# One turn number for every piece of work in place of one lag for each kind: 16 sequences through two transformer-like layers

## The chip, the cores and the metric

One core of a Trainium2 chip runs the whole program. The metric is device time in microseconds from launch to the last store. Three runs of the kernel before gave 691.0, 694.92 and 696.01 us, median 694.92.

## The reference, cut to what matters

Sixteen sequences of 128 tokens and 256 channels pass one after another, independent of each other, through two layers, all in f32.

```
# layer 0: self attention, cross attention over the encoder states, MLP
x = x + attention(qkv(ln1(x)), mask_self) @ w_ao + b_ao          # 16 heads of 16
x = x + attention(q(ln2(x)), kv(enc), mask_cross) @ w_co + b_co
x = x + gelu(ln3(x) @ w1 + b1) @ w2 + b2                          # 256 -> 1024 -> 256
# layer 1: a recurrent layer with 32 heads of 8 channels and an 8 x 8 state for each head
xn = ln(x); sx = token_shift(xn)
w, k, v, r, g = five mixtures of xn and sx, each through its own product
for each token t:                                                  # 128 steps
    a = k[t] (outer) v[t]
    out[t] = r[t] . (u * a + s);  s = a + exp(-exp(w[t])) * s
x = x + (group_norm(out) * gn_w + gn_b) * silu(g) @ Wo.T
x = x + sigmoid(xr @ Wr.T) * (square(relu(xk @ Wk.T)) @ Wv.T)     # xk, xr: mixtures of ln(x) and its shift
```

## The kernel before

All weights and all sixteen sequences lie in SBUF. The work of one sequence is cut into 223 pieces, functions that each issue a few instructions of one engine with the semaphore waits that they need: `a_...` pieces are the two attentions (arg 0 is self, 1 is cross), `b_...` pieces are the MLP and the products of the recurrent layer up to its inputs, `d_...` pieces are the recurrence, its norm, and the last gated MLP. Names carry an argument, as `a_maxima (1, 2)`: cross attention, head group 2.

Each of the engines (SP is the DMA queue, then PE, DVE, ACT, POOL) works through a static list. Its order is software pipelined over sequences: `SP_ORDER` (L87), `PE_ORDER` (L89), `DVE_ORDER` (L100), `ACT_ORDER` (L119), `POOL_ORDER` (L133) each hold (piece, argument, lag), and in round i of `for i in range(B + LAG)` every entry issues its piece for sequence i - lag, if there is such a sequence. So one order holds for all rounds; the first and last rounds are the same list with entries left out. Six or so sequences are in flight at once. An engine executes in its list's order, so a piece that waits holds up all that stand behind it.

A few pieces differ at the ends. Values are spread over the 8 state rows through DRAM for sequences 0 to 13 (`LAST = 2`), and by matmuls with selection matrices (`b_select`, TensorE) for 14 and 15. Roots of the group norm are Newton steps on VectorE for 0 to 13 and `Sqrt` on ScalarE for 14 and 15. `KEEP_WARM` (L78) puts extra matmuls in front of named pieces of the first and last sequences.

The pieces that matter for the change, for one sequence b:

- `b_turn` 1 (TensorE, L675, matmul at L545) turns the normalised row `B_N` that `b_normal` 1 (VectorE, L917) wrote; ScalarE's `b_scale` 1, GpSimd's `b_shift` and VectorE's `b_mixed` lead on to the products.
- `b_valgate` 0 and 1 (TensorE, L750) compute values and gate once ScalarE's `b_keyrec` (L1346) has emptied the bank; `b_values` (ScalarE, L1366) copies the values to `VC`, `b_gatetanh` (L1372) takes the gate's tanh.
- `b_vstore` (L494) writes `VC` to DRAM, `b_vspread` (L499) waits until that has landed and reads it back 8 times over into `V8`, two DMAs of 512 KB. `b_wspread` (L508) waits for `b_decays` (ScalarE, L1359) and copies the decays `EW` 8 times over into `W8`, two DMAs of 512 KB. The profile shows these tiles as `V` and `W`. `a_load` fetches an encoder sequence, `d_store` stores a result. All are on one queue, SP's.
- `d_outer` 0 and 1 (VectorE, L1040) wait for `V8` and form the outer products `AJ`; `d_scan` (scan, L1057) runs the recurrence and needs `W8`; `d_rstate` (L1069 on VectorE for half 0, L1540 on GpSimd for half 1) multiplies by r.
- `b_sum` (L1012) adds the MLP's result, then come the statistics and `b_normal` 1 of the next sequence.
- `d_root_of` (L1403, `Sqrt`, then a one-element `Tanh`), `b_decays` of the last sequence (`Exp`, then a one-element `Sqrt`), and `d_affine` (L1425). The one-element activations are there to load ScalarE's function tables early.

```
            def b_vspread(b, _):
                if b < B - LAST:
                    sp.wait_ge(b_vst, 16 * b + 16)
                    sp.wait_ge(d_a, 2 * b)
...
            def b_wspread(b, _):
                sp.wait_ge(b_ew, b + 1)
                sp.wait_ge(d_s, 2 * b)
```

In the steady order before, SP's round is: spread of values of sequence n, store of n-2, spread of decays of n+1, store of values of n+1, load of n+4.

Of the kernel before, what the change touches and what calls it, by code (L numbers as in the profile page):

```python
# [56 lines left out]
for _name, _n in COLS:  # L57
# [42 lines left out]
DVE_ORDER = [  # L100
    ("a_mask", (0, 1), 1), ("b_streams", 0, 4), ("a_prob_copy", (1, 1), 3), ("d_own", 0, 5),
    ("a_addmask", (0, 1), 1), ("b_streams", 1, 4), ("a_inverse", 1, 3), ("b_streams", 2, 4), ("a_maxima", (0, 0), 1),
    ("d_output", 0, 5), ("a_prob_copy", (1, 3), 3), ("d_means", 0, 5), ("d_centre", 0, 5), ("a_mask", (0, 2), 1),
    ("a_normal", 1, 2), ("d_spread", 0, 5), ("d_guess", 0, 5), ("a_mask", (0, 3), 1), ("d_guess", 1, 5),
    ("d_guess", 2, 5), ("a_maxima", (0, 1), 1), ("d_newton", (0, 0), 5), ("d_newton", (0, 1), 5),
    ("d_newton", (0, 2), 5), ("d_newton", (1, 0), 5), ("d_newton", (1, 1), 5), ("a_stats", 0, 0),
    ("d_newton", (1, 2), 5), ("a_moments", 0, 0), ("d_newton", (2, 0), 5), ("a_context", 1, 3),
    ("d_newton", (2, 1), 5), ("a_maxima", (0, 2), 1), ("a_addmask", (0, 3), 1), ("a_key", 1, 2),
    ("d_newton", (2, 2), 5), ("a_normal", 0, 0), ("d_inverse", 0, 5), ("d_norm", 0, 5), ("d_ruk", 0, 4), ("a_sum", 1, 3),
    ("b_stats", 0, 3), ("b_moments", 0, 3), ("a_query", 1, 2), ("a_maxima", (0, 3), 1), ("d_gated", 0, 5),  # L110
    ("b_normal", 0, 3), ("b_gate", 0, 4), ("a_mask", (1, 0), 2), ("a_mask", (1, 1), 2), ("a_mask", (1, 2), 2),
    ("d_sum", 0, 5), ("a_prob_copy", (0, 1), 1), ("a_mask", (1, 3), 2), ("d_stats", 0, 5), ("a_maxima", (1, 0), 2),
    ("a_addmask", (1, 3), 2), ("d_moments", 0, 5), ("a_maxima", (1, 1), 2), ("a_maxima", (1, 2), 2),
    ("d_outer", 0, 4), ("d_normal", 0, 5), ("d_scan", 0, 4), ("b_sum", 0, 3), ("b_stats", 1, 3),
    ("a_prob_copy", (0, 3), 1), ("a_inverse", 0, 1), ("a_key", 0, 0), ("b_moments", 1, 3), ("d_shift", 0, 5), ("d_mixed", 0, 5),
    ("a_maxima", (1, 3), 2), ("b_normal", 1, 3), ("d_rstate", 0, 4), ("d_mixed", 1, 5), ("d_outer", 1, 4),
    ("a_context", 0, 1), ("a_query", 0, 0), ("b_mixed", 0, 3), ("d_scan", 1, 4), ("d_relu2", 0, 5), ("d_mixing", 0, 5), ("d_final", 0, 5), ("a_sum", 0, 1),
    ("a_stats", 1, 1), ("a_mask", (0, 0), 0), ("a_moments", 1, 1), ("d_rstate", 1, 4)]
# [14 lines left out]
POOL_ORDER = [  # L133
    ("d_final", 0, 6), ("a_addmask", (0, 0), 1), ("b_addnorm", 0, 4), ("b_addnorm", 1, 4), ("b_addnorm", 2, 4),
    ("a_root", 1, 2), ("a_addmask", (0, 2), 1), ("a_addbias", 0, 1), ("a_root", 0, 0), ("a_addbias", 1, 2),
    ("b_root", 0, 3), ("b_addbias", 0, 3), ("a_addmask", (1, 0), 2), ("a_addmask", (1, 1), 2),
    ("a_addmask", (1, 2), 2), ("d_gates", 0, 5), ("d_root", 0, 5), ("d_shift", 0, 5), ("b_root", 1, 3), ("b_shift", 0, 3),
    ("d_rstate", 0, 4)]
# [1498 lines left out]
```

## Time and profile before

| | |
|---|---|
| runs | 691.0, 694.92, 696.01 us |
| profiled execution, first to last instruction | 694.0 us |
| TensorE busy | 645.3 us (93%), 5877 matmuls |
| VectorE busy | 598.2 us (86%) |
| ScalarE busy | 571.7 us (82%) |
| GpSimd busy | 311.6 us (45%) |
| DMA queue of SP | 24.7% of 16 engines' span |

The span is one profiled execution; no launch time is reported beside it. The busy tenths of the page show three parts: a ramp up to about 140 us, a plateau to about 550 us in which TensorE reads 9 in every slice with VectorE and ScalarE at 9 too, and a ramp down. A busy share of TensorE is not a share of its peak, since matmuls are pipelined and their ends are modelled.

### The profile page before, as it was taken

The page shows a single profiled execution, that of the slowest core. Times are in us where ns is not written, and L with a number is a line of the kernel's source. Part 1 is how long each engine was busy: PE and PEld are TensorE (multiplying, and loading weights), DVE is VectorE, ACT ScalarE, POOL GpSimd, SP SyncE. Part 2 cuts the span into 40 slices and gives each one's busy share as a digit, 9 for nine tenths or more (in the row PEclk, how much of TensorE's full clock was granted, in tenths as well). Part 3 has the DMA queues.
Part 4 walks back from the last instruction along what each step waited for, and adds up shares of the span by engine and source line. Part 5 has one row for each costly group of instructions (what it writes and reads, how often), then busy time and mean ns, then how long its engine had stood idle before and what let it go on. Part 6 is the DMA issues. An engine that isn't in the chain of part 4 may idle for free.

```text
span 694.0 us, 17297 instructions
## 1 busy us (share of the span) xinstructions
PE 645.3 (93%) x5877; PEld 561.6 (81%) x5877; DVE 598.2 (86%) x1430; ACT 571.7 (82%) x2071; POOL 311.6 (45%) x440
## 2 busy tenths in 40 slices
PE   6878998999999999999999999999999989898776
PEld 5666787888989888988989888989888877687555
DVE  3598588999999999999999999999999987968274
ACT  1568899899999999999999999999999987664513
POOL 1154252646464554636364646454554624432120
PEclk9999999999999999999999999999999999999799
DMA  8920031221305050504122231305050503120200
GB/s 306 325 70 9 2 104 36 70 70 58 88 9 138 1 146 1 145 2 122 25 85 62 67 81 53 93 4 144 1 146 1 146 0 108 31 70 0 69 9 8
DMA packets 53725, 50.44 MB, mean 73 GB/s; under 512 B 6030, under 2 KB 48902, under 8 KB 53254
## 3 DMA queue, kind: packets, MB, share of 16 engines
q1 hardware_dynamic: 53638, 49.34, 24.7%
q8 instruction: 47, 0.77, 0.5%
q14 instruction: 40, 0.33, 0.1%
HBM read 28.62 MB, written 3.93 MB: 47 GB/s over the span
## 4 chain that ended last, share of the span: by engine, by line
PE 80%; DVE 8%; ACT 7%; issue 3%; POOL 1%; DMA 0%; SPq 0%; DVEq 0%; ACTq 0%; POOLq 0%
PE PS_B L552 16%; PE PS_T L654 9%; PE PS_B L694 8%; PE PS_S L552 7%; PE PS_D L559 5%; PE PS_S L625 4%; PE PS_T L662 4%; PE PS_S L559 4%; PE PS_T L559 4%; ACT SC L1291 3%; PE PS_D L800 2%; PE PS_B L703 2%; PE PS_D L552 2%; ACT PT L1301 2%; PE PS_T L545 2%
## 5 line engine op out<-in xcount | busy, mean ns | idle before, releaser
L1291 ACT ACTIVATE SC<-SC,NMX 128x128 f32<-128x128 f32 x512 | 200.0, 398 | 0.2
L1291 ACT ACTIVATION_READ_ACCUMULATOR SC<-SC,NMX 128x1 f32 x512 | 101.0, 197 | 0.0
L654 PE MATMUL PS_T<-CST,SC 128*128 128x128 f32 x512 | 81.3, 281 | 7.7 <-ACT PT L1301 3.6
L976 DVE TENSOR_REDUCE NMX<-SC 128x4 f32<-128x512 f32 x128 | 85.2, 676 | 0.4 <-POOL SC L1499 0.3
L1301 ACT ACTIVATE PT<-PS_T 128x512 f32<-128x512 f32 x120 | 70.8, 590 | 12.7 <-PE PS_T L654 12.7
L654 PEld LDWEIGHTS PS_T<-CST,SC 128*128 128x128 f32 x512 | 56.4, 141 | 26.1 <-ACT PT L1301 12.7
L1057 DVE TENSOR_TENSOR_SCAN SS<-W,AJ 128x1024 f32<-128x1024 f32 x32 | 73.2, 2288 | 0.2
L552 PE MATMUL PS_B<-MX,W 128*128 128x128 f32 x512 | 64.2, 280 | 4.7 <-ACT KR L1350 4.7
L552 PEld LDWEIGHTS PS_B<-MX,W 128*128 128x128 f32 x512 | 61.3, 196 | 4.9 <-ACT KR L1350 4.9
L1499 POOL TENSOR_TENSOR SC<-SC,MADD 128x512 f32<-128x512 f32 x48 | 59.9, 1276 | 6.5 <-DVE SC L956 6.5
L552 PE MATMUL PS_B<-B_LT,W 128*128 128x128 f32 x512 | 61.1, 278 | 1.0 <-ACT B_LT L1231 0.9
L694 PE MATMUL PS_B<-W,HG 128*128 128x256 f32 x256 | 61.9, 385 | 0.0
L552 PEld LDWEIGHTS PS_B<-B_LT,W 128*128 128x128 f32 x512 | 58.4, 192 | 3.2 <-ACT B_LT L1231 1.9
L1501 POOL TENSOR_TENSOR SC<-SC,MADD 128x512 f32<-128x512 f32 x32 | 42.2, 1318 | 40.4 <-DVE SC L956 40.4
L956 DVE TENSOR_TENSOR SC<-PS_S,MASK 128x512 f32<-128x512 f32 x80 | 51.9, 683 | 4.0 <-PE PS_S L625 4.0
L552 PE MATMUL PS_S<-A_LT,W 128*128 128x128 f32 x384 | 51.8, 280 | 1.3 <-DVE SC L967 1.3
L552 PEld LDWEIGHTS PS_S<-A_LT,W 128*128 128x128 f32 x384 | 50.3, 196 | 3.1 <-DVE SC L967 1.5
L1544 POOL TENSOR_TENSOR SS<-SS,KR 128x1024 f32<-128x1024 f32 x14 | 33.1, 2363 | 41.0 <-DVE SS L1057 41.0
L694 PEld LDWEIGHTS PS_B<-W,HG 128*128 128x128 f32 x256 | 46.1, 190 | 5.6
L1536 POOL TENSOR_TENSOR MX<-MX,XN 128x256 f32<-128x256 f32 x80 | 48.4, 634 | 3.1 <-DVE MX L1029 2.9
L1262 ACT ACTIVATE KP<-PS_S,KB,CST 128x128 f32<-128x128 f32 x112 | 46.1, 480 | 0.8 <-PE PS_S L552 0.8
L1029 DVE SCALAR_TENSOR_TENSOR MX<-PS_B,COL,SX 128x128 f32<-128x128 f32 x160 | 44.1, 336 | 0.7 <-PE PS_B L716 0.7
(231 smaller groups left out, 1595.0 us busy)
## 6 DMA issues: line engine op xcount, KB each, us to landing
W<-EW SPq DMA_DIRECT2D x32, 512.0 KB, 4.1
V<-values_by_head SPq DMA_DIRECT2D x28, 512.0 KB, 5.4
W<-in_weights SPq DMA_DIRECT2D x1, 4160.0 KB, 21.0
ENC<-in_enc SPq DMA_DIRECT2D x16, 128.0 KB, 2.3
out<-X SPq DMA_DIRECT2D x16, 128.0 KB, 5.8
X<-in_x SPq DMA_DIRECT2D x1, 1920.0 KB, 15.7
values_by_head<-VC SPq DMA_DIRECT2D x14, 128.0 KB, 1.8
W<-in_weights SPq DMA_DIRECT2D x1, 1280.0 KB, 8.5
```

Of the source, the lines that this page charges most:

```text
L552: last = pe.matmul(dst[:, m * T:(m + 1) * T], w(name, kt, n, lo + m * P, lo + (m + 1) * P), rhs[:, kt, 0:T], start=(kt == 0), stop=(kt == ...
L559: last = pe.matmul(dst, lhs[:, kt, 0:T], w(name, kt, n, lo, lo + C), start=(kt == 0), stop=(kt == CT - 1))
L654: last = pe.transpose(PS_T[:, j * T:(j + 1) * T], SC[:, nr(b, a) % 2, g, j, :], ident)
L694: last = pe.matmul(PS_B[:, 1, 0:C], HG[:, kt, :], w("w2", kt, C, 0, C), start=(kt == 0), stop=(kt == FT - 1))
L956: dve.tensor_tensor(masked, PS_S[:, g], over_heads(mask), ALU.mult).then_inc(a_masked, 1)
L976: dve.tensor_reduce(NMX[:, nr(b, a) % 2, GH * g:GH * g + GH], SC[:, nr(b, a) % 2, g], AX_X, ALU.max, negate=True)\
L1057: dve.tensor_tensor_scan(SS[:, t].rearrange("p d n -> p (d n)"), W8[:, t].rearrange("p d n -> p (d n)"), AJ[:, t].rearrange("p d n -> p (d ...
L1262: last = act.activation(KP[:, par, t, :], keys[:, t * T:(t + 1) * T], ACT.Identity, bias=KB[:, a, par, t:t + 1], scale=CST[:, K_PAR + par: ...
L1291: last = act.activation(SC[:, nr(b, a) % 2, g, j, :], SC[:, nr(b, a) % 2, g, j, :], ACT.Exp, bias=NMX[:, nr(b, a) % 2, h:h + 1], accum_out ...
L1301: act.activation(PT[:, g], PS_T[:, :].rearrange("p (j n) -> p j n", n=T), ACT.Copy)\
L1499: pool.tensor_tensor(SC[:, nr(b, a) % 2, g], SC[:, nr(b, a) % 2, g], over_heads(MADD[:, b % 2, :]), ALU.add).then_inc(a_added, 1)
L1536: last = pool.tensor_tensor(MX[:, i], MX[:, i], XN[:, :, 1:T + 1], ALU.add)
```

## The change

Each order now holds (piece, argument, turn), a position in units of which 10000 are one sequence, and `..._MOVED` holds other turns for named sequences. `in_order` lists all pieces of all sequences of an engine, sorts them by 10000 * b + turn, and the engine runs that list. No piece's instructions change, nor any wait, nor the number of instructions. Only the order on each of the five engines does: of the 800 pieces in TensorE's list 501 are followed by the same piece as before, of VectorE's 1408 it is 397, of ScalarE's 944 it is 266, of GpSimd's 336 it is 94, of SP's 80 it is 17. The functions `build` and its pieces are otherwise as they were. The whole tables have some 250 lines; below are those that the prediction speaks of.

```diff
@@ -84,60 +84,263 @@
     ('d_keyrec', 0, 15): 4, ('d_val', 0, 15): 2}
 
 
+TURN = 10000
+
 SP_ORDER = [
-    ("b_vspread", 0, 4), ("d_store", 0, 6), ("b_wspread", 0, 3), ("b_vstore", 0, 3), ("a_load", 0, 0)]
+    ("a_load", 0, 90000), ("b_vstore", 0, 110006), ("b_wspread", 0, 110008), ("b_vspread", 0, 120002),
+    ("d_store", 0, 170030),
+]
+SP_MOVED = {
+    ("b_vstore", 0): {4: 120002}, ("b_wspread", 0): {13: 110010}, ("b_vspread", 0): {4: 120004, 13: 110008},
+}
 PE_ORDER = [
-    ("a_prob_turn", (1, 0), 3), ("d_own", 0, 5), ("a_prob_turn", (1, 1), 3), ("b_low2", 2, 4), ("d_read", 0, 5),
-    ("a_prob_turn", (1, 2), 3), ("b_decay1", 0, 4), ("d_oturn", 0, 5), ("a_enc_turn", 0, 2),
-    ("a_prob_turn", (1, 3), 3), ("b_decay2", 0, 4), ("b_keyrec", 0, 4), ("b_keyrec", 1, 4), ("a_val", 1, 2),
-    ("a_pv", 1, 3), ("a_turn", 1, 2), ("b_valgate", 0, 4), ("b_valgate", 1, 4), ("a_key", 1, 2), ("a_out", 1, 3),
-    ("a_query", 1, 2), ("d_biasout", 0, 5), ("d_yturn", 0, 5), ("a_prob_turn", (0, 0), 1), ("a_scores", 1, 2), ("a_prob_turn", (0, 1), 1),
...
+    ("a_prob_turn", (1, 3), 31834), ("a_pv", 1, 32646), ("a_out", 1, 33680), ("b_turn", 0, 35500),
+    ("b_mlp1", 0, 36011), ("b_mlp1", 1, 36350), ("b_mlp2", 0, 36414), ("b_mlp2", 1, 36837), ("b_turn", 1, 38504),
+    ("b_low1", 0, 39300), ("b_low2", 0, 39953), ("b_low2", 2, 40568), ("b_decay1", 0, 41096), ("b_decay2", 0, 42046),
+    ("b_keyrec", 0, 42259), ("b_keyrec", 1, 42475), ("b_valgate", 0, 43259), ("b_valgate", 1, 43505),
+    ("b_select", 0, 45938), ("b_select", 1, 47580), ("d_biasout", 0, 49070), ("d_own", 0, 50189),
...
+    ("b_valgate", 1): {4: 43871, 5: 42818, 7: 43286, 13: 43289}, ("b_select", 0): {14: 45300},
...
 DVE_ORDER = [
...
-    ("b_normal", 0, 3), ("b_gate", 0, 4), ("a_mask", (1, 0), 2), ("a_mask", (1, 1), 2), ("a_mask", (1, 2), 2),
-    ("d_sum", 0, 5), ("a_prob_copy", (0, 1), 1), ("a_mask", (1, 3), 2), ("d_stats", 0, 5), ("a_maxima", (1, 0), 2),
-    ("a_addmask", (1, 3), 2), ("d_moments", 0, 5), ("a_maxima", (1, 1), 2), ("a_maxima", (1, 2), 2),
-    ("d_outer", 0, 4), ("d_normal", 0, 5), ("d_scan", 0, 4), ("b_sum", 0, 3), ("b_stats", 1, 3),
-    ("a_prob_copy", (0, 3), 1), ("a_inverse", 0, 1), ("a_key", 0, 0), ("b_moments", 1, 3), ("d_shift", 0, 5), ("d_mixed", 0, 5),
-    ("a_maxima", (1, 3), 2), ("b_normal", 1, 3), ("d_rstate", 0, 4), ("d_mixed", 1, 5), ("d_outer", 1, 4),
...
+    ("a_query", 1, 24877), ("a_mask", (1, 0), 25126), ("a_mask", (1, 1), 25347), ("a_mask", (1, 2), 25625),
+    ("a_maxima", (1, 0), 25731), ("a_mask", (1, 3), 25963), ("a_addmask", (1, 3), 26651), ("a_maxima", (1, 1), 26768),
+    ("a_maxima", (1, 2), 26990), ("a_maxima", (1, 3), 27259), ("a_prob_copy", (1, 1), 30458), ("a_inverse", 1, 30928),
...
+    ("b_moments", 0, 34830), ("b_normal", 0, 35062), ("b_sum", 0, 37069), ("b_stats", 1, 37292),
+    ("b_moments", 1, 37825), ("b_normal", 1, 38239), ("b_mixed", 0, 38542), ("b_streams", 0, 40167),
+    ("b_streams", 1, 40385), ("b_streams", 2, 40785), ("b_gate", 0, 45064), ("d_ruk", 0, 45741),
+    ("d_outer", 0, 46753), ("d_scan", 0, 46878), ("d_outer", 1, 48106), ("d_rstate", 0, 48205), ("d_scan", 1, 48724),
+    ("d_rstate", 1, 49978), ("d_own", 0, 50246), ("d_output", 0, 50853), ("d_means", 0, 51183),
...
+    ("d_moments", 0, 56301), ("d_normal", 0, 56766), ("d_shift", 0, 57518), ("d_mixed", 0, 57857),
+    ("d_mixed", 1, 58104), ("d_mixing", 0, 58845), ("d_relu2", 0, 59232), ("d_final", 0, 59345),
...
+DVE_MOVED = {
...
+    ("a_maxima", (0, 0)): {0: 9718, 1: 11027, 2: 11234, 7: 10527, 10: 10452, 15: 9955},
+    ("a_mask", (0, 2)): {0: 10064, 1: 10943, 2: 10033, 4: 11395, 11: 10759},
+    ("a_maxima", (0, 1)): {0: 10005, 1: 13332, 4: 11822, 6: 11220, 8: 12231, 10: 12425, 13: 11428, 14: 10963},
...
+    ("d_outer", 0): {1: 46861, 2: 46852, 4: 46770, 6: 45737, 7: 46782, 10: 45512, 11: 46483, 12: 45233, 13: 45238},
...
 ACT_ORDER = [
...
-    ("b_decay2", 0, 4), ("d_squares", 0, 5), ("d_root_of", 0, 5), ("b_decays", 0, 4), ("a_prob_copy", (1, 3), 3), ("a_widen", 1, 3),
-    ("a_exps", (0, 0, 0), 1), ("b_keyrec", 0, 4), ("a_exps", (0, 0, 1), 1), ("a_spread", 1, 3), ("a_scale", 1, 2),
-    ("a_val", 1, 2), ("a_exps", (0, 1, 0), 1), ("b_values", 0, 4), ("a_exps", (0, 1, 1), 1), ("a_key", (1, 0), 2),
-    ("b_gatetanh", 0, 4), ("a_key", (1, 1), 2), ("d_affine", 0, 5), ("a_prob_copy", (0, 0), 1),
-    ("a_exps", (0, 2, 0), 1), ("b_scale", 0, 3), ("a_exps", (0, 2, 1), 1), ("a_prob_copy", (0, 1), 1),
...
+    ("b_gelu", 1, 39068), ("b_scale", 1, 41102), ("b_low", 0, 42105), ("b_decay1", 0, 43968), ("b_decay2", 0, 44908),
+    ("b_keyrec", 0, 45579), ("b_decays", 0, 45745), ("b_values", 0, 46311), ("b_gatetanh", 0, 47062),
+    ("d_first_states", 0, 47504), ("d_own", 0, 52944), ("d_ocopy", 0, 53611), ("d_squares", 0, 54314),
+    ("d_root_of", 0, 54619), ("d_root", 0, 57114), ("d_affine", 0, 57472), ("d_scale", 0, 59537),
+    ("d_keyrec", 0, 61599), ("d_relu2", 0, 61656),
...
+ACT_MOVED = {
...
+    ("a_exps", (0, 2, 0)): {0: -49992, 1: 16360, 2: 16422, 3: 17707, 15: 16587}, ("a_prob_copy", (0, 1)): {13: 19045},
...
+    ("b_decays", 0): {2: 47494, 4: 45557, 5: 45575, 6: 47409, 14: 45106, 15: 43203},
...
+    ("d_root_of", 0): {14: 54145},
+    ("d_affine", 0): {0: 57507, 1: 57601, 2: 57601, 3: 57601, 5: 57601, 6: 57601, 7: 57604, 8: 56444, 11: 56569,
+        12: 54801, 13: 55066, 14: 54391},
...
+    ("d_first_states", 0): {0: 43836, 1: 48302, 2: 47951, 3: 48109, 4: 48734, 6: 47735, 10: 43634, 12: 42669},
...
-LAG = max(lag for order in (SP_ORDER, PE_ORDER, DVE_ORDER, ACT_ORDER, POOL_ORDER) for _, _, lag in order)
...
+def in_order(order, moved):
+
+    turns = [(TURN * b + moved.get((name, arg), {}).get(b, turn), name, arg, b)
+             for name, arg, turn in order for b in range(B)]
+    return [(name, arg, b) for _, name, arg, b in sorted(turns, key=lambda t: t[0])]
...
-        def run(pieces, order, i):
-
-            for name, arg, lag in order:
-                if 0 <= i - lag < B:
-                    pieces[name](i - lag, arg)
+        def run(pieces, order, moved):
+
+            for name, arg, b in in_order(order, moved):
+                pieces[name](b, arg)
...
-            for i in range(B + LAG):
-                run(pieces, SP_ORDER, i)
+            run(pieces, SP_ORDER, SP_MOVED)
```

## Rows read from the trace of the kernel before

**Rows 1.** the page's fourth part: shares of the chain that ended last, by engine

```profile
PE 80%; DVE 8%; ACT 7%; issue 3%; POOL 1%; DMA 0%; SPq 0%; DVEq 0%; ACTq 0%; POOLq 0%
```

**Rows 2.** three stretches: busy us and instructions of PE, PEld, DVE, ACT, POOL; clock, DMA share, GB/s

```profile
0.00:140.00 140.00, 117.91 (x1061) 99.19 (x1061) 102.53 (x241) 102.97 (x400) 54.34 (x81) 1.00 0.35 115
140.00:550.00 410.00, 408.63 (x3902) 362.12 (x3906) 395.48 (x968) 390.05 (x1433) 214.16 (x298) 1.00 0.25 68
...
630.00:694.00 64.00, 45.74 (x303) 38.03 (x302) 36.27 (x74) 21.39 (x48) 10.55 (x18) 0.89 0.08 23
```

**Rows 3.** pieces of the chain of waits: start us, us, engine, output, line

```profile
329.32 3.65 PE PS_B L552 x32
...
366.54 3.65 PE PS_B L552 x32
```

**Rows 4.** ScalarE in time in one sequence's turn: start us, us, line, operation

```profile
360.23 0.40 ACT L1370 ACTIVATE VC<-PS_B 128x256 f32<-128x256 f32 x1
```

**Rows 5.** the DMA queue in time in that turn: start us, us of issuing

```profile
355.40 1.36 SPq L512 DMA_DIRECT2D W<-EW  x2
360.65 0.38 SPq L497 DMA_DIRECT2D values_by_head<-VC  x1
...
362.44 1.20 SPq L505 DMA_DIRECT2D V<-values_by_head  x2
```

**Rows 6.** stretches of 1 us, the columns of rows 2

```profile
357.00:358.00 1.00, 1.00 (x33) 0.80 (x24) 0.92 (x4) 1.00 (x5) 0.22 (x1) 1.00 1.14 343
366.00:367.00 1.00, 1.00 (x9) 0.87 (x8) 1.00 (x4) 1.00 (x6) 1.00 (x2) 1.00 1.00 238
```

**Rows 7.** the two value transfers of that turn, from issue to landing

```profile
DMA to landing us min/median/max: 4.7/5.4/6.1
```

**Rows 8.** VectorE in time, one turn: idle time before a row in brackets

```profile
331.97 1.25 DVE L976 TENSOR_REDUCE NMX<-SC 128x4 f32<-128x512 f32 x2
333.13 1.22 DVE L1050 TENSOR_TENSOR AJ<-V,KR 128x1016 f32<-128x1016 f32 x1
...
337.25 0.42 DVE L1015 TENSOR_TENSOR X<-PS_B,X 128x256 f32<-128x256 f32 x1 [0.38 <-PE PS_B L694]
...
339.58 0.41 DVE L910 TENSOR_SCALAR B_N<-X,B_MV,B_RS 128x256 f32<-128x256 f32 x1
339.90 1.22 DVE L1073 TENSOR_TENSOR SS<-SS,KR 128x1024 f32<-128x1024 f32 x1
341.04 0.61 DVE L1193 SCALAR_TENSOR_TENSOR XR<-SM,COL,XM 128x128 f32<-128x128 f32 x2
```

**Rows 9.** TensorE in time, the same turn

```profile
341.55 0.38 PE L545 MATMUL PS_B<-CST,B_N 128*128 128x128 f32 x2
...
358.20 1.95 PE L552 MATMUL PS_B<-MX,W 128*128 128x128 f32 x16
```

**Rows 10.** ScalarE in time near the end

```profile
647.28 1.28 ACT L1407 ACT_TABLE_LOAD   x1
...
648.88 1.28 ACT L1410 ACT_TABLE_LOAD   x1
...
650.29 0.40 ACT L1362 ACTIVATE EW<-DW 128x254 f32<-128x254 f32 x1
650.70 1.28 ACT L1364 ACT_TABLE_LOAD   x1
...
652.11 0.58 ACT L1350 ACTIVATE KR<-PS_B 128x512 f32<-128x512 f32 x1
```

**Rows 11.** TensorE in time near the end

```profile
652.74 3.78 PE L552 MATMUL PS_B<-MX,W 128*128 128x128 f32 x16 [4.75 <-ACT KR L1350]
```

**Rows 12.** a stretch of 1 us near the end, the columns of rows 2

```profile
654.00:655.00 1.00, 1.00 (x6) 1.00 (x6) 0.00 (x0) 0.00 (x0) 0.00 (x0) 0.50 1.16 351
```

**Rows 13.** VectorE in time near the end

```profile
659.34 0.42 DVE L1161 SCALAR_TENSOR_TENSOR YT<-PS_D,G 128x256 f32<-128x256 f32 x1 [6.19 <-ACT PS_D L1431]
...
662.29 1.22 DVE L1050 TENSOR_TENSOR AJ<-PS_S,KR 128x1016 f32<-128x1016 f32 x1
```

More of the change, by code:

```diff
@@ L133 @@
-POOL_ORDER = [
[L134 to L138, printed above, removed]
-LAG = max(lag for order in (SP_ORDER, PE_ORDER, DVE_ORDER, ACT_ORDER, POOL_ORDER) for _, _, lag in order)
+    ("a_load", 0, 90000), ("b_vstore", 0, 110006), ("b_wspread", 0, 110008), ("b_vspread", 0, 120002),
@@ new lines @@
+PE_MOVED = {
+    ("a_key", 0): {5: 7401, 6: 6834, 12: 7616, 14: 6559, 15: 7442},
+    ("a_val", 0): {1: 8656, 2: 8935, 3: 8789, 4: 8753}, ("a_query", 0): {5: 7342, 12: 7218},
+    ("a_scores", 0): {3: 9634}, ("a_prob_turn", (0, 1)): {2: 15595, 15: 15754},
+    ("a_prob_turn", (0, 2)): {3: 15526, 10: 16391, 15: 16056},
+    ("a_prob_turn", (0, 3)): {4: 17361, 5: 16912, 11: 17302, 15: 16806}, ("a_enc_turn", 0): {2: 19994, 15: 15981},
+    ("a_val", 1): {2: 23969, 3: 23958, 10: 23508, 14: 23613, 15: 23293},
+    ("a_turn", 1): {1: 23042, 4: 22709, 6: 23661, 7: 22778, 10: 23504},
+    ("a_key", 1): {4: 22646, 8: 23791, 13: 23703, 15: 16946}, ("a_prob_turn", (1, 0)): {1: 29710, 15: 27640},
+    ("a_prob_turn", (1, 2)): {1: 30597}, ("a_prob_turn", (1, 3)): {14: 31876},
+    ("a_pv", 1): {0: 32904, 3: 32281, 5: 33472, 7: 32877, 12: 33319},
+    ("a_out", 1): {5: 33899, 7: 33899, 12: 33899, 14: 33291}, ("b_turn", 0): {13: 35666},
[3 rows of a table added]
+    ("b_keyrec", 0): {13: 41863}, ("b_keyrec", 1): {2: 42276}, ("b_valgate", 0): {4: 43579, 5: 42816, 11: 43329},
+    ("b_valgate", 1): {4: 43871, 5: 42818, 7: 43286, 13: 43289}, ("b_select", 0): {14: 45300},
+    ("d_oturn", 0): {14: 52255}, ("d_yturn", 0): {14: 53468}, ("d_out", 0): {13: 55308},
+    ("d_turn", 0): {10: 57347, 13: 56572},
+}
@@ new lines @@
+POOL_ORDER = [
+    ("a_root", 0, 1334), ("a_addmask", (0, 0), 9542), ("a_addmask", (0, 2), 10990), ("a_addbias", 0, 15027),
+    ("a_root", 1, 21604), ("a_addmask", (1, 0), 24645), ("a_addmask", (1, 1), 25899), ("a_addmask", (1, 2), 26941),
+    ("a_addbias", 1, 28837), ("b_root", 0, 34180), ("b_addbias", 0, 35760), ("b_root", 1, 37535),
+    ("b_shift", 0, 38837), ("b_addnorm", 0, 40190), ("b_addnorm", 1, 40351), ("b_addnorm", 2, 42260),
+    ("d_rstate", 0, 49195), ("d_root", 0, 56429), ("d_shift", 0, 56766), ("d_final", 0, 64083), ("d_gates", 0, 90000),
+]
@@ L864, in _ @@
                            d_own, d_read, d_oturn, d_yturn, d_biasout, d_out, d_turn, d_keyrec, d_val)
-            for i in range(B + LAG):
-                run(pieces, PE_ORDER, i)
+            run(pieces, PE_ORDER, PE_MOVED)
         @block.vector
@@ L1216, in _ @@
                            d_moments, d_mixed, d_mixing)
-            for i in range(B + LAG):
-                run(pieces, DVE_ORDER, i)
+            run(pieces, DVE_ORDER, DVE_MOVED)
         @block.scalar
@@ L1454, in _ @@
                            b_gatetanh, d_first_states, d_own, d_ocopy, d_squares, d_root_of, d_root, d_affine, d_scale, d_keyrec, d_relu2)
-            for i in range(B + LAG):
-                run(pieces, ACT_ORDER, i)
+            run(pieces, ACT_ORDER, ACT_MOVED)
         @block.gpsimd
@@ L1569, in _ @@
                            d_rstate, d_gates, d_root)
-            for i in range(B + LAG):
-                run(pieces, POOL_ORDER, i)
+            run(pieces, POOL_ORDER, POOL_MOVED)
 def kernel(**inputs):
```

203 lines of the change are left out of this document (178 added, 25 removed), and 3 rows, old and new, of the table PE_MOVED.

## The prediction

> **What bounds the kernel.** I read the shares of the chain first: TensorE holds 80% of it [rows 1]. Then three stretches of the span: from 140 to 550 us TensorE is busy 408.6 of 410 us, while it idles 22.1 us of the first 140 and 18.3 us of the last 64 [rows 2]. VectorE (395.5) and ScalarE (390.1) are nearly full in the plateau too, so an order that makes either wait can make it the bound. The same matmul group starts at 329.32 and 366.54, a period of 37.2 us for a sequence [rows 3]. No order can gain much there: 1.4 us is idle in all. What an order can gain lies at the ends; what it can lose lies in the plateau, once for each sequence.
>
> The plateau holds because transfers land just in time. I followed one sequence. ScalarE copies the values at 360.23 and is done at 360.6 [rows 4]. The queue had issued the decay spread at 355.40, long before; the store of the values follows at 360.65, their spread at 362.44, both halves issued by 363.6 [rows 5]. The slower half lands 6.1 us after its issue [rows 7], so at 363.0 + 6.1 = 369.1. `d_outer` 0 of that sequence starts one period after its row at 333.13, at 370.3 [rows 8]. Slack here: 1.2 us. From `d_outer` on, VectorE reaches `b_normal` 1 (339.58, done 340.0) and TensorE's `b_turn` 1 starts at 341.55 [rows 8, 9]: slack 1.5 us. In between VectorE waited 0.4 us for `b_sum`, which can be eaten too. The whole loop from `b_turn` 1 through `b_valgate`, values, transfers, `d_outer` and back to `b_turn` 1 so has 3.1 to 3.2 us to spare.
>
> **The change, part by part.** No instruction is added; every cost is a shift of one.
>
> *Transfers in the plateau.* For 12 of the 14 sequences that spread through DRAM (all but 4 and 13) the queue's order is now values stored, decays spread, values spread. ScalarE's `b_decays` also moves behind `b_keyrec`, for sequences 2, 6 and 13 behind `b_values`. So the decays' 1 MB, which ran from 357 on alone at 343 GB/s and a DMA share over 1 [rows 6], is issued at 361.1 and moves just ahead of the values' 1 MB, which itself fills the DMA engines (share 1.00 at 238 GB/s) [rows 6]. Counted from the end of the values' copy: decays issued at +0.4, on the engines at +1.7 (they took 1.3 to start), done at +4.8 (1.05 MB at 343 GB/s is 3.1); the values' own traffic began at about +3.0 before. That is 1.8 us late; allowing a little overlap I take 1.7. Bounds: 0.45 if the two overlap wholly (two more issues, 1.36 us, less the 0.9 that the queue spent waiting for the store to land) [rows 5], 3.1 if all of it adds. `b_values` itself comes 0.3 us later behind moved exponentials. The landing so moves by 2.0, to 371.1.
>
> The Trainium skill, "DMA: Bandwidth & Descriptors", section on two DMAs through the same engine, says that descriptors of one queue start in order but are pipelined. By it the values stay behind the decays, and reads of one may overlap writes of the other. No row shows two such transfers at once.
>
> *VectorE's order in the plateau.* `a_maxima` (1,1) and (1,2) go behind `d_outer` 0: two pieces of 0.6 us [rows 8], so VectorE gets there 1.2 us earlier and then waits for the landing. Between `d_outer` 0 and `b_normal` 1 now stand also these two, the second `d_mixed` (0.5 us from start to start) and `d_rstate` 0 (1.1) [rows 8]: 2.8 us more. Going through the lists with these durations gives +2.3 to +2.8 for sequences 3 and 5 to 10, +1.4 to +1.8 for 2, 4, 11 and 12. The waits of each loop then exceed its slack by 2.0 + 2.3 - 3.15 = 1.2 us on average over the ten sequences 2, 3 and 5 to 12 (sequence 4 keeps the early decays). TensorE's `b_valgate` 1 shifts by one key product, 0.9 us, in five of them, four later and one earlier; part of that hides behind ScalarE's shift. Sum over the plateau: +11 us, with TensorE waiting at `b_turn` 1 and VectorE 2 us at `d_outer` 0 in each. By the bounds: overlap whole gives 0 to 0.3 a sequence, +1; all of it adding gives +24.
>
> *The tail.* After the last sequence's decay input, ScalarE before did `Sqrt` table load, root, `Tanh` load, `b_decays`, `Sqrt` load, then `b_keyrec` at 652.11 [rows 10]; TensorE waited 4.75 us for it and then ran its 16 products in 3.78 us, where the plateau takes 1.95 [rows 9, 11]: the granted clock had fallen to 0.50, the lower level of 1.2 GHz, after that idle time [rows 12]. Now `b_decays` comes first and its early `Sqrt` load serves `d_root_of` of sequence 14 as well, behind `b_keyrec`. Ahead of the copy stand 0.4 (decays), 1.4 (load and its one element) and 0.4 (squares, like the decays' row) from 646.9: it starts at 649.1, 3.0 us earlier. With 1.8 us of idle time in place of 4.75 I expect the clock to hold: 1.8 us more. `d_affine` of 14, for which VectorE waited 6.19 us [rows 13], no longer stands behind the values and a `Tanh` load of 1.3 us. As `d_outer` 0 of 15 (662.29) [rows 13] comes behind that piece's chain, this 1.3 us counts too. Together -6.1, I take -6. Bounds: -3.0 if the clock falls all the same and the rest is covered, -8 if `d_affine` gains its place before the values in full.
>
> A load is 1.28 us and the next operation starts 1.30 after it [rows 10]. The Trainium skill, "ScalarE: Activation LUTs", section "What ACT_TABLE_LOAD costs", has 1.28 plus 1.38 of drain. By that each of the two loads saved would be worth 2.66 and the tail 2 to 3 us more; the rows show no drain, and I go by them.
>
> *The head.* In the first sequence VectorE takes each maximum at once, waiting for GpSimd's mask, and puts the next sequence's statistics last; ScalarE does the first halves of three groups before it closes group 0, so the first transposes of probabilities start some 2 us later, the last about as before. Later sequences of the ramp lie closer to their data. I have no row that prices this; 22.1 us of idle time bounds the gain and few pieces move on TensorE. I take 0, bounds -4 to +3.
>
> **Sum.** 11 - 6 + 0 = +5 against this execution's 694.0 us, and since that is 0.9 under the median of 694.9, 700 us by the median. A change under 1%, 7 us, can't be told from none here.
>
> **Rivals.**
>
> *The transfers are covered* (0.28). If decays and values overlap on the DMA engines, the landing is 0.5 to 1 late, and the loop's 3.15 us just hold 2.3 + 0.75. For: the new VectorE order fits a landing at 369.1 exactly. Against: both transfers show a full share alone [rows 6]. Then only the ends count: 694.9 - 6 = 689 us.
>
> *The ends give more* (0.14). Transfers covered, and the ramps, free of the plateau's order, lose a quarter of their 40 us of idle time [rows 2] instead of 6: 683 to 685 us. For: the pieces of the first and last sequences move most. Against: on TensorE they hardly move.
>
> *VectorE becomes the bound outright* (0.13), the side above 1% slower. If the values land 3.1 us late, VectorE, which has 14.5 us idle in 410 [rows 2], 1.3 a sequence, must stand 3.2 us at `d_outer` 0, and each sequence costs 2 to 2.4 us: +20, less the tail's 6, 709 us. It decides from a landing later than 371.5 in that turn's clock. Against: it takes no overlap at all and a late store.
>
> **Numbers.** The forecast has 0.45 and holds 695 to 706 by its own bounds, a third of it over 702. Faster by over 1% (under 688): 0.14 from the ends and 0.12 of the covered case, 0.26. Slower by over 1% (over 702): 0.13 and 0.14 of the forecast, 0.27. Within: 0.47. The range 685 to 707 leaves out most of the two outer cases.
>
> **What would show it.** Right: a period near 38.4 us between equal matmul groups in the plateau; VectorE idle about 2 us before `d_outer` 0 with a DMA as releaser; a TensorE wait for `B_N` of over 1 us a sequence; the decay spread issued after the value store, values landing over 10 us after their copy, not 8.5; two table loads fewer and `KR`'s wait under 2 us near the end with the clock at 1.00. Wrong: a period still 37.2 with the values landing 0.5 us later means the transfers overlap; a wait that ends with another releaser means that another moved piece decides.

## The result, and the profile after

The changed kernel takes 738.93 us (median of four, 736.21 to 741.97); the kernel before, run beside it, 693.69. The ratio is 1.064, 95% interval 1.060 to 1.069. Forecast were 700 us and a range up to 707: the sign was right, the size of the plateau's loss was wrong by a factor of four.

The profiled execution has a span of 737.2 us against 694.0. The queue issues the first and the last of the 14 value stores at these times, first before, then after (start us, us of issuing):

```profile
99.52 0.39 SPq L497 DMA_DIRECT2D values_by_head<-VC  x1
...
584.06 0.38 SPq L497 DMA_DIRECT2D values_by_head<-VC  x1
```

```profile
98.05 0.38 SPq L699 DMA_DIRECT2D values_by_head<-VC  x1
...
630.44 0.38 SPq L699 DMA_DIRECT2D values_by_head<-VC  x1
```

They cut the span into a head (99.5 us before, 98.1 after), 13 periods (484.5, 532.4) and a rest (109.9, 106.8). The whole loss lies in the periods: +47.9, against -1.5 and -3.1. A period is 40.95 us in the mean, not 37.3.

The chain of waits of the changed kernel, shares by engine [rows 1], then the stretches [rows 2]:

```profile
PE 38%; DVE 20%; DMA 11%; issue 10%; ACT 9%; SPq 6%; POOL 5%; DVEq 0%; ACTq 0%; POOLq 0%
```

```profile
0.00:140.00 140.00, 119.39 (x1067) 100.71 (x1071) 103.25 (x240) 103.56 (x399) 54.84 (x80) 0.98 0.33 108
140.00:550.00 410.00, 380.79 (x3536) 330.70 (x3529) 371.07 (x878) 357.57 (x1298) 210.84 (x269) 0.99 0.22 60
```

TensorE idles 29 us of 410 where it idled 1.4. The chain, 80% on TensorE before, now runs through every engine and the transfers. These waits of that stretch (us in total, times, longest us) are not in the list of the kernel before at all:

```profile
DVE AJ L1250 <- DMA V<-values_by_head: 23.8, 9, 3.8
...
PE PS_D L746 <- DVE D_N L1110: 16.1, 7, 2.9
...
ACT RW L1506 <- DVE RINV L1188: 9.4, 6, 3.1
...
PE PS_B L746 <- DVE B_N L1110: 6.5, 8, 2.6
```

One turn shows the waits that were forecast, and longer ones than forecast. First ScalarE in time, the decays and then the values [rows 4]:

```profile
419.26 0.41 ACT L1561 ACTIVATE EW<-DW 128x254 f32<-128x254 f32 x1
...
421.48 0.38 ACT L1569 ACTIVATE VC<-PS_B 128x256 f32<-128x256 f32 x1
```

The queue in time [rows 5]:

```profile
421.89 0.38 SPq L699 DMA_DIRECT2D values_by_head<-VC  x1
422.36 1.35 SPq L714 DMA_DIRECT2D W<-EW  x2
423.76 0.90 SPq L694 DMA_DIRECT2D out<-X  x1
424.70 1.33 SPq L719 DMA_DIRECT2D ENC<-in_enc  x1
426.13 2.10 SPq L707 DMA_DIRECT2D V<-values_by_head  x2
```

The second half of the values' spread in the chain of waits (start us, us):

```profile
427.63 6.30 DMA V<-values_by_head
```

VectorE [rows 8], then TensorE:

```profile
434.06 1.22 DVE L1250 TENSOR_TENSOR AJ<-V,KR 128x1016 f32<-128x1016 f32 x1 [2.90 <-DMA V<-values_by_head]
435.19 0.68 DVE L1176 TENSOR_REDUCE NMX<-SC 128x4 f32<-128x512 f32 x1
435.79 0.40 DVE L1110 TENSOR_SCALAR D_N<-X,D_MV,D_RS 128x256 f32<-128x256 f32 x1
```

```profile
436.25 0.44 PE L746 MATMUL PS_D<-CST,D_N 128*128 128x128 f32 x2 [2.48 <-DVE D_N L1110]
```

The values' spread is issued 4.2 us after their store, not 1.8, its second half 5.7, not 2.4 [rows 5]; it lands at 433.9, 12.0 us after the store's issue, not 8.5. This is one of the later landings: over sequences 2 to 12 the slower half lands 11.2 us after the store's issue in the mean, before 8.6. The decays move first, at the old rate, then the values at theirs [rows 6], with a thinner stretch between the two:

```profile
425.00:426.00 1.00, 1.00 (x19) 0.66 (x12) 0.97 (x4) 1.00 (x5) 0.83 (x3) 1.00 1.14 340
428.00:429.00 1.00, 1.00 (x11) 1.00 (x11) 1.00 (x3) 0.98 (x4) 1.00 (x1) 1.00 0.56 113
430.00:431.00 1.00, 1.00 (x12) 1.00 (x11) 1.00 (x3) 1.00 (x5) 1.00 (x2) 1.00 1.03 238
```

So the two do not overlap, but they were not put to the test either: the values' spread was issued when the decays' traffic was nearly over.

VectorE stands still for 2.9 us, and `d_normal`, which has nothing to do with the values, stands behind it in VectorE's list, so TensorE waits too.

A second thing is in the page's first part. Both kernels execute the same 1430 VectorE and 440 GpSimd instructions, yet VectorE is busy 19 us longer (598.2 before) and GpSimd 27 us (311.6 before):

```profile
PE 657.1 (89%) x5877; PEld 566.3 (77%) x5877; DVE 617.4 (84%) x1430; ACT 574.4 (78%) x2069; POOL 338.4 (46%) x440
```

The tail gained what was forecast. ScalarE in time, TensorE in time, a stretch in the columns of rows 2, and VectorE in time [rows 10 to 13]:

```profile
695.87 0.41 ACT L1561 ACTIVATE EW<-DW 128x254 f32<-128x254 f32 x1
696.30 1.28 ACT L1563 ACT_TABLE_LOAD   x1
...
698.01 0.58 ACT L1549 ACTIVATE KR<-PS_B 128x512 f32<-128x512 f32 x1
```

```profile
698.64 1.16 PE L753 MATMUL PS_B<-MX,W 128*128 128x128 f32 x8 [1.33 <-ACT KR L1549]
...
700.07 1.06 PE L753 MATMUL PS_B<-MX,W 128*128 128x128 f32 x8
```

```profile
699.20:704.00 4.80, 4.78 (x37) 4.31 (x36) 2.56 (x8) 2.64 (x7) 0.00 (x0) 1.00 0.74 241
```

```profile
701.11 0.43 DVE L1361 SCALAR_TENSOR_TENSOR YT<-PS_D,G 128x256 f32<-128x256 f32 x1 [1.37 <-ACT PS_D L1630]
```

### The profile page after: what moved, and what is told of

Read it like the earlier page. It is cut to its first block, busy times and chain, and to the rows that moved or that the text cites. A ratio compares the mean times of both kernels' runs of the same rounds, so it can differ in the third digit from the quotient of the medians.

```text
span 737.2 us, 17295 instructions
## 1 busy us (share of the span) xinstructions
PE 657.1 (89%) x5877; PEld 566.3 (77%) x5877; DVE 617.4 (84%) x1430; ACT 574.4 (78%) x2069; POOL 338.4 (46%) x440
## 4 chain that ended last, share of the span: by engine, by line
PE 38%; DVE 20%; DMA 11%; issue 10%; ACT 9%; SPq 6%; POOL 5%; DVEq 0%; ACTq 0%; POOLq 0%
DMA V<-values_by_head 10%; PE PS_B L753 5%; PE PS_T L855 4%; ACT SC L1490 3%; PE PS_D L760 3%; PE PS_S L753 3%; PE PS_T L863 2%; DVE NMX L1176 2%; PE PS_S L826 2%; PE PS_B L904 2%; DVE SS L1257 2%; SPq L714 2%; PE PS_B L895 2%; PE PS_T L760 2%; PE PS_D L1001 2%
## 5 line engine op out<-in xcount | busy, mean ns | idle before, releaser
L895 PE MATMUL PS_B<-W,HG 128*128 128x256 f32 x256 | 63.8, 397 | 0.0
L1250 DVE TENSOR_TENSOR AJ<-V,KR 128x1016 f32<-128x1016 f32 x28 | 35.6, 1278 | 32.7 <-DMA V<-values_by_head 32.7
L1666 POOL TENSOR_SCALAR B_RS<-B_MV 128x1 f32<-128x1 f32 x32 | 10.0, 312 | 109.6 <-DVE B_MV L1096 109.5
L895 PEld LDWEIGHTS PS_B<-W,HG 128*128 128x128 f32 x256 | 48.9, 200 | 6.1
```

Of the source, the lines that this page charges most:

```text
L895: last = pe.matmul(PS_B[:, 1, 0:C], HG[:, kt, :], w("w2", kt, C, 0, C), start=(kt == 0), stop=(kt == FT - 1))
```

## The experiments

Each run is timed beside the kernel before, which gave 693.3 to 694.4 us. An old list is put in place of a new one like this, with `X` for the engine and `X_LAGS` for its table of before:

```
+X_ORDER = [(name, arg, TURN * lag + 10 * k) for k, (name, arg, lag) in enumerate(X_LAGS)]
+X_MOVED = {}
```

Not every mixture can run: the new lists of TensorE and ScalarE lean on each other, and on those of VectorE and GpSimd, so that such a mixture would deadlock. GpSimd's new list alone, or all new but VectorE's, could not be tried. The queue's and VectorE's new lists together, without GpSimd's, would run and were not tried.

**One list at a time.**

The queue's new, all others old:

> The kernel before, with the queue's new order alone (decay spread, output store and encoder load ahead of the value spread); all four engines keep their old order. Theory Q (the late value spread is the main cause): landing about 3.5 us later than before, 12 us after the values' copy, slack of the loop 3.1; 715 to 730 us, VectorE waiting 2 us or more at d_outer 0 in the middle sequences. Theory O (the engines' new orders are the main cause, the queue adds little): under 702 us. Between: both are needed.

708.55 us, ratio 1.023 (1.018 to 1.028). The queue alone costs 15 us, 1.14 us for each of the 13 periods (100.09 to 599.42). VectorE's wait for the values appears, 16.3 us in ten times. Neither theory holds the number; the queue's share is a third.

The queue's old, all others new:

> The changed kernel with the queue's old order alone (decay spread ahead of the value store, output store before both); all four engines keep the new order. Theory Q: the wait of VectorE for the values goes, period back near 37.5 us, 690 to 700 us. Theory O: the engines' order keeps most of the loss, over 720 us. Queue and VectorE together (each tips the other over): 700 to 712 us.

741.28 us, 1.069 (1.066 to 1.073): nothing comes back. Theory Q as stated falls. The 13 periods take 532.2 us (99.99 to 632.16), as in the changed kernel. The queue in time, one turn of this run, shows why its order was the wrong handle:

```profile
420.31 1.35 SPq L711 DMA_DIRECT2D W<-EW  x2
422.50 0.38 SPq L696 DMA_DIRECT2D values_by_head<-VC  x1
422.92 0.75 SPq L716 DMA_DIRECT2D ENC<-in_enc  x1
425.52 1.84 SPq L704 DMA_DIRECT2D V<-values_by_head  x2
```

The decays are first in the queue again, but ScalarE's new order makes them ready only 2.2 us before the values (419.87 and 422.09; before, 5.3 us), so their 1 MB now moves ahead of the store, and the spread waits 3.0 us for the store to land instead of 1.8. Over sequences 2 to 12 the values land 10.0 us after the store's issue in the mean, so about half of their delay is gone, and no time with it. That shows already that the time does not follow the landing alone.

VectorE's new, all others old:

> The kernel before, with VectorE's new order alone (d_outer 0 ahead of two maxima, d_normal behind it; queue, TensorE, ScalarE and GpSimd as before). Theory Q: the landing stays where it was, VectorE waits about 1 us for it, loop slack of 3 us covers most: 694 to 702 us. Theory O: TensorE waits for the normalised input behind d_outer 0, over 710 us.

716.64 us, 1.033 (1.029 to 1.037). 23 us, with no wait for the values at all. Of them 15.7 lie in the 13 periods (102.45 to 602.65), 1.2 us each. The prediction's shift of 2.3 us by VectorE's list lies inside its slack of 3.15 and should have cost nothing alone.

Only the tail's three pieces:

> The kernel before, with three pieces of ScalarE moved at the very end: b_decays of the last sequence ahead of the squares of the one before, d_root_of and d_affine of that one behind b_keyrec. If the tail's gain stands by itself: KR copied 3 us earlier, granted clock up in its products, 5.8 us gained, 688 to 689 us. If the gain of the changed kernel's tail came from its late plateau instead: 693 to 695 us.

```
+ACT_MOVED = {("b_decays", 0): {15: 190275 - 150000}, ("d_root_of", 0): {14: 190345 - 140000},
+             ("d_affine", 0): {14: 190347 - 140000}}
```

688.45 us, 0.993 (0.991 to 0.995). The tail's gain stands by itself, 5.2 us. ScalarE, then TensorE in this run:

```profile
645.74 0.41 ACT L1375 ACTIVATE EW<-DW 128x254 f32<-128x254 f32 x1
...
647.88 0.58 ACT L1363 ACTIVATE KR<-PS_B 128x512 f32<-128x512 f32 x1
```

```profile
648.51 2.05 PE L567 MATMUL PS_B<-MX,W 128*128 128x128 f32 x16 [1.68 <-ACT KR L1363]
```

**Transfers, and what stands behind the wait.**

```
 # queue's old list, and
+ACT_MOVED[("b_decays", 0)] = {b: ACT_MOVED[("b_decay2", 0)].get(b, 44908) + 1 for b in range(B)}
```

> The changed kernel with the queue's old order and b_decays put directly behind b_decay2 on ScalarE, so that the decays' 1 MB moves ahead of the value store again; all else of the four engines keeps the new order. Theory C (the collision of the two transfers needs only one of queue and ScalarE, and costs the same through either): values land 8.5 to 9 us after their copy, VectorE's waits for them fall under 1 us a sequence, about 15 us come back, 720 to 727 us. Theory E (the engines' new order has so much in the loop that the landing hardly counts): over 733 us.

725.52 us, 1.046 (1.042 to 1.049): 13 us back, as theory C has it. VectorE's waits for the values fall from 22.9 to 5.1 us between 150 and 550 us. The chain of waits of this run now goes through GpSimd (start us, us):

```profile
418.86 0.72 POOL X L1681
419.58 0.74 POOL X L1712
420.32 3.69 POOL SC L1697 x3
...
424.10 1.04 POOL D_RS L1666
...
425.22 0.56 POOL D_RS L1668
```

Two bias additions and three masks stand ahead of the root that `d_normal` waits for.

```
+for b in range(2, 10):
+    DVE_MOVED[("d_outer", 0)][b] = 46992      # behind d_normal and both maxima
+    DVE_MOVED[("d_scan", 0)][b] = 46994
```

> The changed kernel with d_outer 0 and d_scan 0 of sequences 2 to 9 put behind d_normal and both maxima on VectorE; nothing else moved. Theory N (what costs is that d_normal stands behind the wait for the values, so TensorE waits at d_turn): TensorE's 18 us of waits for D_N go, VectorE does 1.5 to 2 us of other work inside the wait, 8 sequences, 723 to 731 us. Theory L (the loop through the landing and b_normal 1 sets the period, whatever is done inside the wait): D_N's wait goes but TensorE waits at b_turn 1 instead, 735 to 740 us.

733.78 us, 1.056 (1.052 to 1.059). TensorE's wait for `D_N` falls from 16.1 to 3.1 us, its wait for `B_N` rises to 7.6; 5 us come back, between the two theories. `d_normal` behind the wait was a small part.

TensorE and ScalarE old, the rest new; then the queue old as well:

> TensorE and ScalarE in the old order, queue, VectorE and GpSimd in the new one. If the costs of the queue's order (15 us, measured alone) and of VectorE's (23 us) add: 728 to 735 us, and TensorE's and ScalarE's orders add little. If they share one slack of the loop they cost less together than apart, 718 to 726 us, and TensorE's and ScalarE's orders carry the rest of the 45 us.

> Queue, TensorE and ScalarE in the old order, VectorE and GpSimd in the new one. If GpSimd's order is the match of VectorE's and gives back what VectorE's order alone lost (its wait for B_RS): 700 to 708 us. If VectorE's own order is the loss: 713 to 720 us as with VectorE alone. If GpSimd's adds: over 722 us.

751.05 us (1.083, 1.076 to 1.091) and 733.88 (1.058, 1.055 to 1.061). The first lies above both ranges expected. So GpSimd's new list adds 17 us to VectorE's, the queue's adds 17 more, and TensorE's and ScalarE's new lists give 12 back. By the first and last value store of one profiled execution each, the 13 periods take:

| new lists | 13 periods, us | more than the line above |
|---|---|---|
| none | 484.5 | |
| VectorE | 500.2 | 15.7 |
| and GpSimd | 512.2 | 12.0 |
| and the queue | 531.8 | 19.6 |
| all | 532.4 | 0.6 |

Added in this order the three make up the plateau's whole loss (the queue's list alone costs 14.8 us of periods), so they do not share one slack; what TensorE's and ScalarE's lists give back lies at the ends. The shares hold for this order of adding only: with all other lists new, the queue's list gives nothing back.

**Which pieces?** I took five of VectorE's (theory P) and two of GpSimd's.

```
+for b in range(3, 10):
+    DVE_MOVED[("d_outer", 0)][b] = 46992
+    DVE_MOVED[("d_normal", 0)][b - 1] = 56993
+    DVE_MOVED[("d_scan", 0)][b] = 46994
+for b in range(2, 12):
+    DVE_MOVED[("d_rstate", 0)][b] = 48260
+    DVE_MOVED[("d_outer", 1)][b] = 48335
```

> VectorE in the new order, all else old, as in the run that gave 716.6 us, but in sequences 3 to 9 d_outer 0, d_normal and d_scan 0 stand behind both maxima again, and in sequences 2 to 11 d_rstate 0 and d_outer 1 stand behind b_normal 1. Theory P (these products of two tiles in SBUF, put right behind the moments, hold up GpSimd's inverse root of one column: 27 us of GpSimd and 9 us of VectorE ran over their usual length there, 3 and 1 in the kernel before, and D_N and B_N came late): overlong operations fall to under 12 us on GpSimd, 702 to 709 us. Theory R (the loss comes from the many other small moves of VectorE): over 712 us.

719.53 us, 1.039 (1.034 to 1.043): nothing gained (716.6 without it). Putting these five pieces back does not bring the time back. GpSimd is busy 9 us less (326.1 against 335.3 us), so a part of the mutual hold-ups went, and it was not on the path. More than half of them stayed (311.6 before), where theory P had expected more than half to go, so the hold-ups themselves are not cleared.

```
+POOL_MOVED[("a_addbias", 0)].update({b: 13400 for b in range(3, 14)})
+POOL_MOVED[("a_addbias", 1)] = {b: 23990 for b in range(2, 14)}
```

> VectorE and GpSimd in the new order, all else old, as in the run that gave 733.9 us, but GpSimd's two bias additions (a_addbias 0 and 1) stand ahead of b_root 0 again, as before. If these two, of 0.73 us each with a root ahead of them, are what delays the three masks and d_root in GpSimd's new order (17 us between the runs with and without it): 718 to 726 us. If it is the rest of GpSimd's order: over 730 us.

730.99 us, 1.054 (1.051 to 1.058): 3 of 17 us. The two additions are a small part.

> The changed kernel with the transfers put back as before (725.5 us) and VectorE's five pieces put back as in the run beside this one; TensorE, ScalarE and GpSimd in the new order. Theory P, by the gain of theory P alone: 712 to 718 us. If GpSimd's order now sets D_N by itself, so that VectorE's pieces don't matter: 722 to 727 us.

> As the one before, and GpSimd's two bias additions ahead of b_root 0 too. If transfers, VectorE's pieces and GpSimd's additions are the whole of the loss but for the sequences left as they are: 701 to 710 us. If more is lost elsewhere: over 715 us.

733.19 (1.057) and 729.0 us (1.050), against 725.5 without either. VectorE's five pieces, put back where they used to stand among others that stand elsewhere, made it worse by 8 us, above both ranges expected; GpSimd's two additions on top gave 4 of them back.

**GpSimd's long operations taken away.** Additions cut like this, in all three places:

```
-pool.tensor_tensor(X[:, b, :], X[:, b, :], row("b2"), ALU.add)
+pool.tensor_tensor(X[:, b, 0:8], X[:, b, 0:8], row("b2")[:, 0:8], ALU.add)
```

> The changed kernel with GpSimd's mask and bias additions cut to 8 elements each (it leaves out most of these additions; same instructions, orders and waits). Theory G (what VectorE's and GpSimd's new orders lose is lost between the two: a root or a subtraction queued behind masks, and operations of one held up by the other's): 715 to 722 us, GpSimd's and VectorE's overlong operations under half. Theory V (VectorE's own many small moves and the transfers): over 732 us.

> The kernel before with the same additions of GpSimd cut to 8 elements (leaves out most of them). Both theories: GpSimd is never what is waited for in the middle, 691 to 695 us; the difference to the run beside it is then the change's loss without GpSimd's long operations.

728.48 us for the changed kernel (1.049, 1.045 to 1.053) and 694.0 for the one before (1.000, 0.997 to 1.002). 10 us come back, between the theories; before, GpSimd's operations cost nothing.

> The changed kernel with the transfers put back as before and GpSimd's additions cut to 8 elements (leaves out most of them). Measured singly these gave 13 and 10 us. If they add: 713 to 718 us, and what is left of the loss, about 22 us, is VectorE's own order, as the 23 us of VectorE's order alone say. If transfers and GpSimd hold up the same thing: 722 to 726 us.

705.92 us, 1.017 (1.012 to 1.022). Transfers and GpSimd's operations, singly worth 13 and 10 us, are worth 33 together, more than either range expected. Each covers the other: with the transfers mended the chain goes through GpSimd (above), and with GpSimd short VectorE still waits 27.0 us for the values. What is left over the cut kernel before is 12 us.

> The kernel before with VectorE's new order alone and GpSimd's additions cut to 8 elements (leaves out most of them). If VectorE's new order loses by itself, through its own pieces taken too early and too late: 710 to 717 us, as without the cut (716.6). If it loses through GpSimd (the two engines holding each other up, masks late): 695 to 702 us.

709.17 us, 1.022 (1.018 to 1.026). Of the 23 us that VectorE's list costs alone, 7.5 come through GpSimd's long operations and 15 do not. These 15 still hold a rival: with the same short operations GpSimd is busy 222.1 us here and 202.8 in the cut kernel before, so its small operations are still held up. In the run before this one it is 224.9 us, beside the 12 us that were left there.

**The slack itself, and the ramp.**

```
+                if arg == (1, 3) and 3 <= b < 13:
+                    dve.tensor_reduce(EXTRA[:, b, :], SC[:, nr(b, a) % 2, g], AX_X, ALU.max, negate=True)
```

> The kernel before with one more VectorE reduction of 0.67 us (a copy of the fourth maximum into an unused tile) in each of the sequences 3 to 12; the result is the same. If VectorE's 1.3 us of idle time a sequence is slack, as the prediction took it: 694 to 696 us, period 37.2 us. If nothing in the period is slack for a shift of VectorE: 0.6 us for each of ten, 699 to 701 us.

697.99 us, 1.006 (1.003 to 1.008): 4 us for ten operations of 0.6 us. The period goes from 37.21 to 37.53, by two value stores of the queue in this run:

```profile
362.99 0.38 SPq L498 DMA_DIRECT2D values_by_head<-VC  x1
...
400.52 0.38 SPq L498 DMA_DIRECT2D values_by_head<-VC  x1
```

Half of each small operation comes through, between the two theories, although VectorE idled 1.3 us a period.

```
+    new = in_order(order, moved)[:int(0.12 * B * len(order))]
+    return new + [piece for piece in old if piece not in new]
```

> The first 12% of every engine's list in the new order, all that follows in the old order, and the three moved pieces of ScalarE at the end. If the ramp's gain of 1.5 us in the changed kernel stands by itself: 686 to 688 us. If it came from elsewhere or the passage between the orders costs as much: 688 to 690 us, as with the tail alone.

694.84 us, 1.001 (interval 0.9995 to 1.0033), 6 us slower than the tail alone and above both ranges expected. The passage between the orders costs 4.4 us in its first period (101.42 to 143.46 us, 42.0, where before has 37.7), and the first store comes later, not earlier. The ramp's 1.5 us can't be had this way.

The tail alone, 688.45 us, is the fastest version found and beats both kernels.

## Why the prediction was wrong

**Transfers: the right order, the delay in another place.** Counted from the values' copy, the landing moved 3.6 us in the turn shown and 2.5 in the mean of sequences 2 to 12, where the forecast has 1.7 (its 2.0 less the 0.3 that the copy itself is late). The forecast priced the decays' traffic, with the values moving right behind it, 4.8 us after their copy. The decays' fast traffic does end about then (427, 5 us after the copy), but the values fill the DMA engines only from 429 on, since they were issued late. Of the 3.6 us, 3.3 have passed before the spread's second half is issued; from there it takes 6.3 us to land, 6.1 before. I counted the decays' two issues, but passed over `d_store`, which from sequence 6 on stands between the decays' and the values' spread as well (0.90 us), and took the other issues at their old length (the encoder load takes 1.33 us here and 0.9 to 1.0 in most turns, 0.47 before; the spread's first half 1.46, 0.60 before). Why issues last longer, and whether two such transfers overlap when they are issued together, no run shows. The queue's list alone has the same landing (11.1 us in the mean) and costs 1.14 us a period.

**One slack for all: the failed step.** "The waits of each loop then exceed its slack by 2.0 + 2.3 - 3.15 = 1.2 us" sets both shifts against one slack. The slack was read along one loop of one turn, each wait with its own cover. Shifts of 2.3 us by VectorE's list or 2.5 by the landing should each have vanished in 3.15 alone. But VectorE's list alone, with the values on time, costs 1.2 us a period (102.45 to 602.65 us) and 6 us at the ends, and the queue's list alone 1.14. One more operation of 0.6 us lengthens the period by 0.32. An engine idle 1.3 us a period had no slack of 1.3 us. My reading of this is that pieces of three engines wait for each other at many points, and a piece that is late at any of them is paid for; the runs show the costs, not these points one by one.

**GpSimd: left out, the second failed step.** It was idle more than half the time, and no step of the sum priced its list, whose pieces moved furthest of the four engines (5.9 places in the mean; 1.4 to 2.5 on the others). It costs 17 us on top of VectorE's, and cutting GpSimd's long additions alone gives 10 us back. That next to nothing waited for it before was a property of the old order, not of the engine.

**Interplay.** Transfers and GpSimd's operations end in the same stretch, `d_outer` 0 and `d_normal`. In the whole change each hides the other: 13 and 10 us singly, 33 together. A sum term by term, as mine, can't show that. That the forecast had the right sign is in part luck: its one cost in the plateau, +11 us, stood for three that are 47 us together.

**What was seen rightly.** Decays issued after the value store, values late, VectorE standing at `d_outer` 0 with a DMA as releaser (2.6 us each in nine turns; forecast 2), TensorE waiting for `B_N` (0.8 us each in eight turns; forecast over 1), and the rival on the slower side, with 709 us, still 30 too fast. A wait for `D_N` was not named, though `d_normal` stood right behind the moved piece.

**The tail: right in its sum and in the first two terms.** `KR` comes 2.8 us after `DW`, not 5.9 (-3.1, forecast -3.0); TensorE waits 1.33 us; the products take 2.2 us in place of 3.78 at a granted clock of 1.00, not 0.50; VectorE waits 1.37 for the affine, not 6.19, and gets to it 3.1 us after `KR`, not 7.2: 4.1 us gained where 3.1 were forecast, of which 1.4 are lost again before the end. From `DW` to the end 42.0 us against 47.8: -5.8, forecast -6. The Trainium skill, "ScalarE: Activation LUTs", section "What ACT_TABLE_LOAD costs", adds 1.38 us of drain to each load; an estimate from it would have the gain 2 to 3 us larger. This trace does not agree: the next operation again starts 1.30 us after the load (696.30, 697.60), and the measured gain is the one without a drain.

**The head** gave 1.5 us, within the bounds; the 0 had no row behind it.

**Open.** The 12 to 15 us that are left with GpSimd's operations short are not traced to pieces: the five that I suspected did not bring them back, and VectorE's list differs from the old one by two places in the mean, in each sequence in another way. GpSimd's small operations, still held up by about 20 us in these runs, are a rival that no run took away. Whether a list that repeats alike in every sequence would lose as much was not tried, since the new turns made alike in the plateau deadlock.

## What to carry over

- Where three engines run above 95%, treat every moved piece as priced, and don't net two shifts against a slack read along one path; measure the slack by adding one small operation.
- Price the idle engine's list too. An engine that nothing waits for can become the bound by order alone.
- Here the end was separable and the steady state was not: the three pieces at the end gave their full 5 us alone, while VectorE's five pieces put back into a foreign order made it worse.

## What the hardware showed

VectorE and GpSimd hold each other up, operation by operation. GpSimd's power of a single column takes 0.55 or 0.56 us in all 79 cases of the kernel before. With VectorE's list alone 7 of the 79 take 0.87 to 1.67 us. Here VectorE multiplies two SBUF tiles at that time. GpSimd in time, then VectorE:

```profile
389.32 1.67 POOL L1555 TENSOR_TENSOR B_RS<-B_RS,CST 128x1 f32<-128x1 f32 x1
```

```profile
389.37 1.22 DVE L1160 TENSOR_TENSOR SS<-SS,KR 128x1024 f32<-128x1024 f32 x1
```

And with both new lists VectorE's normalisation, 0.41 us [rows 8], takes 1.35 and ends 0.15 us after GpSimd's mask. GpSimd, then VectorE:

```profile
390.46 1.27 POOL L1609 TENSOR_TENSOR SC<-SC,MADD 128x512 f32<-128x512 f32 x1
```

```profile
390.53 1.35 DVE L1022 TENSOR_SCALAR D_N<-X,D_MV,D_RS 128x256 f32<-128x256 f32 x1
```

The Trainium skill, "SBUF — State Buffer", section "SBUF: two separate sides", says that the two share a port pair as an exclusive lock for a whole instruction; it counts for a VectorE operation in a two-port mode, or for one with two SBUF inputs against a GpSimd one that reads SBUF, and whichever starts first gets it. The first pair agrees in that one waits for the other: GpSimd's power ends 0.40 us after VectorE's product. It does not agree in the order, since GpSimd's row starts 0.05 us earlier; starts on GpSimd are rough in a profile. In the second pair GpSimd is first and VectorE waits, as the rule has it, if `D_N` is in such a mode, which no row tells. The sum is not small: with equal instructions VectorE and GpSimd together are busy 46 us longer in the changed kernel, 6 us with the queue's list alone. How much of the 45 us these hold-ups cost is not settled: the run that removed a part of them gained nothing, and none removed them all.
